# A graph-attention and expert kernel: earlier gathers across block borders, the plan of the items kept on chip, table preparation moved beside the third group of gathers

## What is computed

```python
ft = (layernorm(x) @ W).reshape(n, 4, 64)
e = leaky_relu(e_src[src] + e_dst[dst], 0.2)        # one score per head
ex = exp(e - segment_max(e, dst)[dst])
a = ex / segment_sum(ex, dst)[dst] * dist
x = x + segment_sum(ft[src] * a, dst)
# then 6 experts of three 256x256 layers, the best two of a router, softmax weighted
x = x + experts(layernorm(x))
```

## Time and profile before

| quantity | value |
|---|---|
| median of three runs | 3129.61 us |
| the three runs | 3122.08, 3132.09, 3129.61 us |
| the profiled execution, its own time | 3125.72 us |
| its span, first to last instruction | 3124.0 us |
| TensorE busy | 2332.9 us (75%) |
| VectorE busy | 1824.0 us (58%) |
| ScalarE busy | 1467.0 us (47%) |
| GpSimd busy | 2095.2 us (67%) |
| mean granted TensorE clock | 0.869 |

### The profile page before, as it was taken

One profiled execution on the slowest core, in us unless ns is written; L12 is line 12 of the kernel. 1 busy time (PEld: TensorE's weight loads), 2 busy tenths in 40 slices (PEclk: granted clock), 3 DMA queues, 4 the chain that ended last, 5 costly groups with the idle time before them and its releaser, 6 DMA issues. The chain is left out here.

```text
span 3124.0 us, 62545 instructions
## 1 busy us (share of the span) xinstructions
PE 2332.9 (75%) x15568; PEld 1888.6 (60%) x15569; DVE 1824.0 (58%) x4215; ACT 1467.0 (47%) x2676; POOL 2095.2 (67%) x2064
## 2 busy tenths in 40 slices
PE   4946667767777777777777777777739999899995
PEld 3725555555556555666565666656637877777774
DVE  6855444555566666677777777777769333332232
ACT  2513223334444454455555666556625554444442
POOL 0046777777777777777777776666406777777775
PEclk9966777877878888889989998988869999999997
DMA  5645555555655666666666656555550445455443
GB/s 173 193 120 152 161 159 163 173 171 168 175 173 173 177 180 176 184 188 183 191 183 178 186 179 182 169 171 163 136 95 9 82 79 81 77 81 83 79 77 46
DMA packets 231876, 450.52 MB, mean 144 GB/s; under 512 B 55818, under 2 KB 148782, under 8 KB 230769
## 3 DMA queue, kind: packets, MB, share of 16 engines
q0 software_dynamic: 114816, 265.53, 36.5%
q1 hardware_dynamic: 76616, 140.14, 14.1%
q10 hardware_dynamic: 39924, 38.86, 3.8%
HBM read 376.74 MB, written 69.01 MB: 143 GB/s over the span
## 5 line engine op out<-in xcount | busy, mean ns | idle before, releaser
L422 POOL DMA_INDIRECT rows<-table,src_col x1568 | 1505.2, 960 | 559.8 <-issue 460.9
L1376 PE MATMUL m_A<-m_msg,m_by_edge 128*128 128x260 f32 x3920 | 1169.1, 461 | 262.6 <-issue 194.0
L1376 PEld LDWEIGHTS m_A<-m_msg,m_by_edge 128*128 128x128 f32 x3920 | 888.6, 233 | 455.7 <-issue 263.7
L1230 ACT ACTIVATE m_apart<-drow,nid 128x1024 bf16 x297 | 341.0, 1148 | 654.1 <-SPq L963 577.2
L1064 DVE TENSOR_TENSOR m_msg<-rows,m_A 128x2048 f32<-128x2048 f32 (+1 forms) x294 | 568.0, 1932 | 111.4 <-issue 103.4
L1584 POOL DMA_INDIRECT out<-x_con,x_to_i x206 | 329.2, 1598 | 105.8 <-issue 79.8
L1362 PEld LDWEIGHTS m_E<-m_look_parts,m_by_node 128*128 128x128 bf16 x7104 | 231.6, 97 | 271.0 <-issue 234.2
L1362 PE MATMUL m_E<-m_look_parts,m_by_node 128*128 x7104 | 245.3, 167 | 187.6 <-ACT m_by_node L1233 180.8
L1040 DVE TENSOR_TENSOR m_z<-m_E,rows 128x64 f32<-128x64 f32 x295 | 65.7, 223 | 486.2 <-PE m_E L1362 363.1
L1233 ACT ACTIVATE m_by_node<-m_apart,m_one 128x1024 bf16<-128x1024 bf16 x297 | 341.0, 1148 | 9.7
L1026 DVE TENSOR_TENSOR m_by_edge<-m_A,row 128x1024 f32<-128x1024 f32 (+1 forms) x295 | 306.8, 1040 | 0.4 <-issue 0.2
(11 more groups left out here) (246 smaller groups left out, 2257.3 us busy)
## 6 DMA issues: line engine op xcount, KB each, us to landing
drow<-edges SPq DMA_DIRECT2D x196, 512.0 KB
rows<-table,src_col POOLq DMA_INDIRECT x1568
table<-f_rowbuf SPq DMA_DIRECT2D x14, 924.0 KB, 4.9
ydram<-m_y ACTq DMA_DIRECT2D x49, 264.0 KB
m_xb<-in_x ACTq DMA_DIRECT2D x48, 256.0 KB
out<-m_x ACTq DMA_DIRECT2D x48, 256.0 KB
f_xin<-in_x SPq DMA_DIRECT2D x13, 896.0 KB, 7.0
x_w<-in_L_ffn_expert_w SPq DMA_DIRECT2D x18, 256.0 KB, 5.7
```

The costliest lines, as they stand in the source:

```text
L422: nc.gpsimd.indirect_dma_start(K.rows[:, g % RING, j, :], None, table, bass.IndirectOffsetOnAxis(ap=K.src_col[:, g, j:j + 1], axis=0)).the ...
L1230: a.activation(apart[i][:, :], drow[:, bass.ds(g % RING, 1), :].rearrange("p a n -> p (a n)"), ACT.Abs, bias=K.nid[:, bass.ds(b, 1)], scal ...
L1376: m = t.matmul(psA[i][:, 0:MSG], by_edge[i][:, j, :], msg[i][:, j, :], start=(j == tiles[0]), stop=(j == tiles[-1]))
```

## The change

- SyncE no longer waits at the end of `features` for the last two stores of the table; GpSimd waits for them in `edge_tables`, ahead of its first gather.
- The plan has its place in SBUF (`K.plan`, integers) from the start. GpSimd clears it beside VectorE's first instructions, VectorE writes the columns straight into it (float to integer in the same copies), and the cast, the store to DRAM, the load and their waits are gone.
- `split_look` makes the three bf16 parts in `lookup_table`, and ScalarE clears `sums` there (a Copy of a zero that is read 4160 times a partition); both are gone from the head of `main_stage`, whose waits shrink accordingly.
- To make room, `rowbuf` lives longer, and the normalized rows and `wide` lie in the place of `K.rows`.

The seven instructions are the same; the place is not. The core of the diff:

```diff
 def edge_tables
-            sp.wait_ge(asked, 6)
-            sp.dma_start(sched, tab_i[:, :]).then_inc(stored, 16)
-            sp.wait_ge(stored, 16)
...
+            nc.gpsimd.memset(plan[:, :], 0).then_inc(consts, 1)
+            for h in range(2):
+                pool.wait_ge(K.table_stored[h], 16 * (NQ // 2))
             pool.wait_ge(copied, 4)
             for g in range(AHEAD - 1):
                 gather(nc, K, table, g)
...
-            st.did(v.memset(tab[:, :], 0.0))
             dve.wait_ge(consts, 3)
...
+            dve.wait_ge(consts, 4)
             def column(at, words, i, of):
-                st.did(v.tensor_copy(tab[:, at + i:at + words * NW:words], of))
+                st.did(v.tensor_copy(plan[:, at + i:at + words * NW:words], of))
...
-            st.did(v.tensor_copy(tab_i[:, :], tab[:, :]))
-            st.settle()
-            v.nop().then_inc(asked, 1)
 def lookup_table
+        @block.scalar
+        def _(act):
+            act.wait_ge(zeroed, 1)
+            nc.scalar.activation(K.sums[:, :, :], zero[:, :].unsqueeze(2).broadcast_to([P, AR, MSG]), ACT.Copy)\
+              .then_inc(cleared, 1)
+            act.wait_ge(cleared, 1)
...
+            v.memset(zero[:, :], 0.0).then_inc(zeroed, 1)
...
+            split_look(v, st, K)
 def features
-            for h in range(2):
-                sp.wait_ge(stored[h], 16 * (LAST + 1))
             sp.wait_ge(K.edge.stored, 16)
 def main_stage
-            sp.dma_start(plan[:, :], sched).then_inc(plan_in, 16)
...
-            v.memset(sums[:, :, :], 0.0).then_inc(ready, 1)
...
-            st.did(v.scalar_tensor_tensor(rest[:, :, 0:HEADS], ends, SLOPE, bound, ALU.mult, ALU.subtract))
-            st.did(v.tensor_tensor(rest[:, :, HEADS:2 * HEADS], ends, bound, ALU.subtract))
...
-            act.wait_ge(plan_in, 16)
-            act.wait_ge(ready, 5)
+            act.wait_ge(ready, 4)
...
-            pe.wait_ge(plan_in, 16)
-            pe.wait_ge(look_steps, 7)
```

More of the change, by code:

```diff
@@ L308, in _, with split_look, exact_bounds @@
                 v.nop().then_inc(split, 1)
-def exact_bounds(nc, K, table, sched):
+def split_look(v, st, K):
+    rest = K.look_rest[:, :, :]
+    ends, bound = K.look[:, :, 0:HEADS], K.look[:, :, HEADS:2 * HEADS]
+    st.did(v.scalar_tensor_tensor(rest[:, :, 0:HEADS], ends, SLOPE, bound, ALU.mult, ALU.subtract))
+    st.did(v.tensor_tensor(rest[:, :, HEADS:2 * HEADS], ends, bound, ALU.subtract))
+    st.settle()
+    for n in range(3):
+        part = K.look_parts[:, :, 8 * n:8 * n + 8]
+        st.did(v.tensor_copy(part, rest))
+        st.settle()
+        if n < 2:
+            st.did(v.tensor_tensor(rest, rest, part, ALU.subtract))
+            st.settle()
+def exact_bounds(nc, K, table):
     BIG = 3e38
@@ L888, in _, with main_stage @@
                 multiply(2 * it + 1, 1)
[L891 removed]
+def main_stage(nc, K, table, x, ydram, w, out):
     with ExitStack() as ctx:
@@ L1142, in _ @@
             v.tensor_scalar(less_base[:, :], K.base[:, :], -1.0, None, ALU.mult).then_inc(ready, 1)
-            st = Steps(dve, look_steps)
-            rest = look_rest[:, :, :]
-            ends, bound = K.look[:, :, 0:HEADS], K.look[:, :, HEADS:2 * HEADS]
-            st.did(v.scalar_tensor_tensor(rest[:, :, 0:HEADS], ends, SLOPE, bound, ALU.mult, ALU.subtract))
-            st.did(v.tensor_tensor(rest[:, :, HEADS:2 * HEADS], ends, bound, ALU.subtract))
-            st.settle()
-            for n in range(3):
-                part = look_parts[:, :, 8 * n:8 * n + 8]
-                st.did(v.tensor_copy(part, rest))
-                st.settle()
-                if n < 2:
-                    st.did(v.tensor_tensor(rest, rest, part, ALU.subtract))
-                    st.settle()
-            dve.wait_ge(ready, 5)
+            dve.wait_ge(ready, 4)
             v.nop().then_inc(added, 1)
-            dve.wait_ge(plan_in, 16)
             fetch(0, 0)
@@ L1915, in gnn_ffn_kernel @@
         K.lg = sb("lg", [P, NB, NX])
+        K.table_stored = [ctx.enter_context(nc.semaphore(f"table_stored{h}")) for h in range(2)]
         K.rows, K.drow = sb("rows", [P, RING, GT, ROW]), sb("drow", [P, RING, GE])
@@ L1921, in gnn_ffn_kernel @@
         K.dst_col, K.dist_col = sb("dst_col", [P, NG, GT]), sb("dist_col", [P, NG, GT])
[L1922 to L1934 removed]
+        with ExitStack() as middle:
+            sb = lambda n, s, d=F32: middle.enter_context(nc.sbuf_tensor(n, s, d))
+            K.plan, K.sums = sb("plan", [1, PLAN], I32), sb("sums", [P, AR, MSG])
+            K.look_parts, K.look_rest = sb("look_parts", [P, NBD, 24], BF16), sb("look_rest", [P, NBD, 8])
+            with ExitStack() as early:
+                sb = lambda n, s, d=F32: early.enter_context(nc.sbuf_tensor(n, s, d))
+                K.every_second = sb("every_second", [P, NPAIR])
+                K.wcat = sb("wcat", [P, 2, NF])
+                K.scores = sb("scores", [P, NBD, 2 * HEADS])
+                K.edge = EdgeRows(nc, early)
+                K.rowbuf = [sb(f"rowbuf{h}", [P, HB, ROW]) for h in range(2)]
+                constants(nc, K, W, att_src, att_dst, src, dst, dist)
+                features(nc, x, K, table, edges)
+                sort_edges(nc, K, edges, sorted_edges)
+                edge_tables(nc, edges, K, table, w)
+                lookup_table(nc, K, table)
+            exact_bounds(nc, K, table)
+            main_stage(nc, K, table, x, ydram, w, out)
         experts(nc, K, ydram, w, out)
```

60 lines of the change are left out of this document (21 added, 39 removed).

## The result

The changed kernel takes **3113.22 us** (median of ten runs, 3111.15 to 3118.23); the kernel before took 3123.78 us beside it (median of ten runs, 3119.14 to 3132.09, the three shown ahead among them). The ratio is 0.9966, with a 95% interval of 0.9955 to 0.9977: 10.6 us or 0.34% faster, a little over what a measurement of this kernel can tell from no change. The profiled execution took 3118.23 us.

The account below looks back on a forecast made before the run. It took a chain to bound the kernel: the way to group 4's gather, a GpSimd-paced stretch, then item-limited stretches and experts. Terms 3.6 + 3.3 - 1.4 + 3.1 = 8.6 us, off 3127.4, gave 3119 us, range 3109 to 3130.

Parts of the forecast that it names:

- head, paced stretch, item-bound stretch: Whole program: way to group 4's gather (244.44 us), GpSimd-paced gathers to 1680 us, then items limit; gains carry to the end.
- The store's wait: End of `features`: without SyncE's wait for the last table stores the border comes 3.6 us earlier (2.6 to 3.8).
- `tab` and its clearing: `edge_tables`: without VectorE's memset, casts and first gather come 2.3 us earlier; GpSimd's memset, at most 3.5 us, is hidden.
- The rival: `edge_tables`: GpSimd's memset holds VectorE's casts, losing the 2.3 us or slightly more; gain 6.3 us, 3121 us; chance 0.18.
- The cast to integers: End of the 16 gathers in `edge_tables`: without this cast the last gather is undisturbed, 1.0 us gained.
- The split beside the third group: `lookup_table`: VectorE's moved split holds two gathers of the third group, a loss of 1.4 us (0 to 2.6).
- The clearing of `sums`: `lookup_table`: ScalarE's clearing takes an estimated 4.7 us beside 10 us of gathers and costs nothing.
- The head of the main stage: Start of `main_stage`: memset and split gone, ScalarE's load issue is late next; group 4's gather 3.1 us earlier (2.9 to 5.0).
- The other end, 5.0: Start of `main_stage`: if the load's issue doesn't hold ScalarE, group 4's gather comes 5.0 us earlier.
- the quicker head: Main stage's start and third group: shorter load issue or fewer held gathers; gain 11.5 us, 3116 us; chance 0.22.
- the border was not held by another engine: End of `features`: rival that another engine holds the border, so deleting the wait gains nothing; total gain 5.0, 3122 us; chance 0.04.
- the slower end: 1680 to 2245 us: an earlier start lowers TensorE's granted clock to 0.80, costing 20 us; 3139 us; chance 0.06.

Follow-up runs that it names:

- the head made ten microseconds longer: The changed kernel with twelve GpSimd memsets of an unread buffer, each waited for, ahead of group 4's first gather: 3124.32 us, ratio 1.0003.
- the late load: The changed kernel with ScalarE's first load of `m_xb` moved behind its first exponential: 3113.34 us, ratio 0.9967.

## Why the prediction was right, and which term was not

**The time and the sign.** Forecast 3119 us (3109 to 3130), measured 3113.22. The sum was 8.6 us, the measured gain 10.6. The rest of the 5.6 us between the two times is the starting point: I counted from 3127.4, the mean of four executions, and ten give a median of 3123.8. The 0.44 for "faster by over 0.3%" was the case that came, at 0.34%, and by little; the sum had said 0.28%, on the other side of the line. The reading of what bounds the kernel (head, paced stretch, item-bound stretch) is borne out by the head made ten microseconds longer.

**Right in mechanism, but not in sum.** The measured head gained 6.0 us, so 2.6 of the 8.6 did not come, and the 10.6 of the time holds 4.6 us that no term of the sum explains. That the time agrees with the forecast as well as it does is in part luck: a term that failed and a gain that nothing explains lie on opposite sides.

- *The store's wait:* forecast 3.6, measured 3.2 in the change and by itself.
- ***`tab` and its clearing:* this is the step that failed.** "It is hidden, with 1.5 us to spare" looked at where GpSimd's memset ends and not at whom it holds meanwhile. The 2.3 us were lost entirely, and the first gather even came 0.6 us later in its block: this term measured -0.6 and not +2.3. I had the row that seemed to speak against a hold, a cast beside a GpSimd operation, and weighed it above the page of the Trainium skill named above, by which the memset would hold the cast. That row shows two GpSimd operations counted together (x2, 1.55 us), of which the first starts 0.27 us ahead of the cast, and no memset. The cast of 0.26 us beside it does go unheld, and does so in other profiles of the study as well, so not every GpSimd instruction holds every cast; but it said nothing about a memset. The rival had 0.18; with both instructions becoming ready within a tenth of a microsecond it deserved more. Its own sum was 6.3 us, and the head gained 6.0.
- Not in the forecast at all: the first gather lies 4.32 us behind the first copy of `src_col`, and 3.61 before. The last copy of `src_col` ends 0.99 us ahead of it, and 0.29 before. The 0.7 us are the same with the plan cleared in `features` (4.31), so the memset is not their cause. The gather now carries three waits and carried one; whether that costs it was not tried.
- *The cast to integers:* forecast 1.0; the 16 gathers are 1.29 us quicker, 0.99 of it in the last one. The border behind them is 0.4 longer, forecast as nothing. The upper bound, a gain of 1.2 there, is far off.
- *The split beside the third group:* forecast a loss of 1.4 from two gathers held. Only one more was held, 0.77 us, and 0.79 is the loss. A gather that was issued 0.4 us before a subtraction (216.74 against 217.13) was not held by it, and neither was the one at 215.48 by the split's first subtraction. The row at 215.70 that the forecast leaned on the earlier trace rows is an addition and not a subtraction (L670), and the gather it holds was issued 0.06 us ahead of it: it shows a hold that ends with VectorE's instruction, but not that the first comer wins. And the part of the gain that I had put down to the split was none, since it is not the last thing TensorE waits for in either place.
- *The clearing of `sums`:* forecast hidden, 4.7 us long; it is hidden, and 3.67 us long.
- *The head of the main stage:* forecast 3.1, measured 3.27. ScalarE was late next, as said, because of the load's issue; the late load shows it. The other end, 5.0, is 5.6 in that kernel (17.72 to 12.08).

Of the rivals, the quicker head did not come by itself, the border was not held by another engine, and TensorE's clock stayed at 0.88 from 2000 to 2300 us: no run says anything for the slower end.

## What to carry to other kernels

When work is moved to an idle engine, ask not only whether it ends in time there, but which instruction of a neighbour starts while it runs: a GpSimd memset of 2.4 us beside a cast on the critical path makes the first gather 2.1 us late, and 166 us earlier, where no long VectorE instruction stands beside it, it costs nothing that head or time shows. Behind each wait that goes, look for the one that is next, and try it at once: here the load's issue was worth 2.2 us beside the 3.3 that the head of the main stage had gained. And when a gain is smaller than the scatter of the time, measure the distance between two fixed points of the trace (it repeats to 0.03 us here), and prove with one large delay that this distance carries to the end.

## What the runs showed of the hardware that was not expected

- A GpSimd memset holds a VectorE cast from integers to floats for its whole length, although the two have no data in common: cast 2.38 us beside a memset of 2.40, 1.23 beside 1.25, and 0.21 without one. A cast beside GpSimd's TENSOR_SCALAR is not held (0.26 us); what tells the two cases apart was not tested.
- A VectorE instruction with two operands in SBUF can hold a gather that is issued near its start: the subtraction at 219.16 makes it 1.72 us instead of 0.95, ending 0.84 us behind the subtraction (219.16 + 0.98, 219.26 + 1.72), and the addition at 213.80 makes it 1.47, though the gather was issued 0.09 us ahead. A subtraction that starts 0.39 us behind the gather's issue does not, and neither do casts to bf16 of the same 0.98 us.
- Not every such instruction does. The split's first subtraction (215.47, 0.61 us) leaves the gather issued 0.01 us behind it at 0.95, and in the kernel that clears the plan in `features` a gather at 239.18 takes 0.95 us in the midst of the multiply of rows that runs 2.29 us from 238.68. What sets the holding ones apart no run tells.
- The issue of the first load on ScalarE in the main stage takes 2.33 us at the block's start, and 0.44 us where it is issued some nine microseconds into the block.
- A border whose last engine has just issued gathers costs 3.4 to 4.0 us from the last gather's end to the first of the next block in the fourteen profiles, and two borders in a row 4.6 to 4.7.
